# A graph, attention and expert block on one Trainium2 core: a new order in five places where stages meet

## What is computed

```python
xn = _layernorm(x)
x = x + gnn(xn, edge_index) + mix(xn)
x = x + ffn(_layernorm(x))
# gnn: layer_norm, two layers of graph attention (4 heads of 192, 2 heads of 96), then [x, out2] @ Wu + bu
#   e = leaky_relu(s_src[src] + s_dst[dst]); alpha = exp(e - max) / sum; out = sum(alpha * h[src])
# mix: linear attention with 12 heads of 64 (q, k = elu + 1), projection, then an MLP 768-3072-768
# ffn: router on the mean over all tokens, the two best of 4 experts (768-1536-768), gates, layer norm
```

## Time and profile before

| | |
|---|---|
| Runs of the kernel before | 1988.61 to 1995.7 us, median 1988.61 us (3 runs) |
| The profiled execution | 1991.11 us, its span 1989.4 us |
| TensorE busy | 1910.3 us, 96% |
| VectorE busy | 1179.5 us, 59% |
| ScalarE busy | 606.8 us, 31% |
| GpSimd busy | 415.9 us, 21% |
| Granted TensorE clock, mean | 0.981 of full speed |

### The profile page before, as it was taken

How to read it: one execution, slowest core, us unless ns; L and a number is a source line. 1 busy time by engine, 2 the same in 40 slices (tenths; PEclk the granted TensorE clock), 3 DMA queues, 4 the chain that set the end, 5 groups by cost and what they waited for, 6 DMA issues and landing times.

```text
span 1989.4 us, 28296 instructions
## 1 busy us (share of the span) xinstructions
PE 1910.3 (96%) x10979; PEld 1820.2 (91%) x10979; DVE 1179.5 (59%) x2085; ACT 606.8 (31%) x1175; POOL 415.9 (21%) x317
## 2 busy tenths in 40 slices
PE   7999899999789999999999999999989999999997
PEld 4677899999788999879999999999989999999997
DVE  8888569998784423678625334253557435274347
ACT  6533228888774311224401001010341001010013
POOL 1000001210000631133224124041114314043120
PEclk9999999999898999999999999999989999999999
DMA  4322401111123210023112011020232102021013
GB/s 146 118 95 102 132 7 50 60 42 48 74 117 145 87 48 1 25 67 114 55 41 64 16 48 56 9 64 17 66 92 64 40 25 65 9 79 40 25 52 120
DMA packets 76958, 125.50 MB, mean 63 GB/s; under 512 B 3350, under 2 KB 47672, under 8 KB 76830
## 3 DMA queue, kind: packets, MB, share of 16 engines
q1 hardware_dynamic: 73106, 111.22, 17.2%
q10 hardware_dynamic: 3724, 12.54, 1.7%
HBM read 98.30 MB, written 25.45 MB: 62 GB/s over the span
## 4 chain that ended last, share of the span: by engine, by line
PE 79%; DMA 7%; DVE 5%; ACT 4%; issue 2%; SPq 1%; ACTq 0%; POOL 0%; DVEq 0%; POOLq 0%
PE pb L1084 25%; PE pa L670 24%; PE pb L670 9%; PE pa L736 3%; PE pa L850 3%; PE pb L802 3%; PE pb L992 3%; PE pa L836 2%; DMA xg_d<-xw 2%; PE pb L850 2%; DMA xw<-wt_d 2%; DMA xu<-in_x 1%; DMA wt_d<-xu 1%; DMA md_d<-mds 1%; ACT sm L1483 1%
## 5 line engine op out<-in xcount | busy, mean ns | idle before, releaser
L1725 ACT ACTIVATE tr<-pb,V 128x418 f32<-128x418 f32 (+1 forms) x144 | 87.7, 610 | 765.3 <-PE pb L1084 762.5
L1084 PE MATMUL pb<-X_hi,uw_hi 128*128 128x416 f32 (+1 forms) x864 | 305.6, 354 | 3.2 <-DVE uw_lo L2324 3.2
L1084 PE MATMUL pb<-X_hi,uw_lo 128*128 128x416 f32 (+1 forms) x864 | 304.9, 353 | 0.0
L1084 PE MATMUL pb<-X_lo,uw_hi 128*128 128x416 f32 (+1 forms) x864 | 304.8, 353 | 0.0
L670 PE MATMUL pa<-dw_hi,hh 128*125 128x384 f32 x960 | 246.4, 338 | 0.7 <-ACT tr L1725 0.7
L670 PE MATMUL pa<-dw_hi,hl 128*125 128x384 f32 x960 | 245.9, 337 | 0.0
L670 PE MATMUL pa<-dw_lo,hh 128*125 128x384 f32 x960 | 245.9, 337 | 0.0
L2271 DVE CAST hh<-tr 128x418 fp32r<-128x418 f32 (+1 forms) x144 | 116.7, 811 | 202.6 <-ACT tr L1725 202.6
L1229 POOL CAST uw_hi<-raw 128x768 fp32r<-128x768 f32 x47 | 42.8, 911 | 708.8 <-PE pb L1084 612.3
L670 PEld LDWEIGHTS pa<-dw_hi,hh 128*125 128x125 f32 x960 | 172.2, 185 | 1.3 <-ACT tr L1725 1.0
L670 PEld LDWEIGHTS pa<-dw_lo,hh 128*125 128x125 f32 x960 | 172.9, 185 | 0.0
(11 more groups left out here) (396 smaller groups left out, 3547.0 us busy)
## 6 DMA issues: line engine op xcount, KB each, us to landing
raw<-in_L_mix_fc_w SPq DMA_DIRECT2D x48, 384.0 KB, 3.3
raw<-in_L_ffn_w SPq DMA_DIRECT2D x47, 384.0 KB, 3.2
md<-md_d SPq DMA_DIRECT2D x11, 610.4 KB
md_d<-mds SPq DMA_DIRECT2D x10, 610.4 KB
md<-md_d ACTq DMA_DIRECT2D x8, 610.4 KB
raw<-in_L_mix_qkv_w SPq DMA_DIRECT2D x24, 192.0 KB, 4.0
TOK<-in_x SPq DMA_DIRECT2D x10, 375.0 KB
xn_d<-TOK SPq DMA_DIRECT2D x10, 375.0 KB
```

The source lines that it names most:

```text
L1084: last = nc.tensor.matmul(pb[:, j % 4, 0:n], w_[:, kk, :], x_[:, kk, o:o + n], start=(kk == 0 and q == 0), stop=(kk == KT - 1 and q == 2))
L1725: last = A_(RE[f"tr{j % 3}"][:, 0:w], pb[:, j % 4, 0:w], ACT.Identity if func == "mish" else func, bias=bias(b))
```

## The change

It moves work in five places and computes the same values.

1. Edge stage: SyncE issues the load of `xu1` and `graph_tile` earlier in its loop; VectorE does `x_low(0)` after the one-hots of the next tile; the count of turns before a tile is added up in registers rather than loaded (`turns_before`).
2. Between the layers: steps 40 and 41 are done in two parts. `minus_max(s, 0)` on VectorE takes the maximum over the first 1125 columns, two one-column operations; ScalarE makes the weights of those columns with it (`weights_part`, signal `xa`), TensorE transposes and gathers them into a bank of their own (`weights_back_part`, `gather_part`, banks `early_sums`). When the last tile's scores are there, the last 125 columns are done with the final maximum (`tb`, `ev` signal the transpose and its copy), and `denominator_of_both` scales the early sums by a ratio, adds the late ones and takes the reciprocal: three operations.
3. Normed tiles: `xs` 0 and 1 are loaded right after layer 1, 2 and 3 by ScalarE's queue near the end of layer 2, the rest in the key stage; the rows `kvb` are loaded at the last two tiles. All ten are scaled by ScalarE. GpSimd waits for a key product before each page split.
4. Queries: nine jobs stand ahead, `q_sum` comes two jobs behind, the denominators of the first chunk after the eighth query, and GpSimd splits `wp` pages after jobs 5, 7, ... 15.
5. Router: the last tile's sums come from the unnormed tile (`scaled_sums`), and ScalarE copies the expert's page before `y_features(NT - 1)`; the gates are spread after the second expert job.

```diff
--- before.py
+++ after.py
             for t in range(NT):
-                if t >= XFIRST + 2:
-                    graph_tile(t - XFIRST - 2)
+                if t == 3:
+                    sp.wait_ge(*at("bu_ok", 1))
+                    sp.dma_start(RE["xu1"][:], x_t[1]).then_inc(sem("xu_in1"), 16)
                 for u in ln_tiles(t):
                     sp.wait_ge(*at("ln_xn", u + 1))
                     sp.dma_start(xn_d[u], TOK[:, u, :]).then_inc(sem("xn_out"), 16)
                 if t == 1:
                     for u in (0, 2):
                         sp.dma_start(RE[f"xu{u}"][:], x_t[u]).then_inc(sem(f"xu_in{u}"), 16)
-                if t == 3:
-                    sp.wait_ge(*at("bu_ok", 1))
-                    sp.dma_start(RE["xu1"][:], x_t[1]).then_inc(sem("xu_in1"), 16)
+                if t >= XFIRST + 1:
+                    graph_tile(t - XFIRST - 1)
                 sp.wait_ge(*at("e_md", t + 1))
                 sp.dma_start(md_d[t], RM[f"mds{t % 2}"][:]).then_inc(sem(f"md_out{t % 2}"), 16)
                 if t == XFIRST + 1:
                     for k in range(3):
                         rows_page(PG_W1 + k, A["gnn_W1"], k)
 
-            for u in range(NT - XFIRST - 2, NT):
+            for u in range(NT - XFIRST - 1, NT):
...
             sp.wait_ge(*at("at_o", STEPS1))
+            for t in range(2):
+                xs_load(t)
             for t in range(NT):
-                if t == NT - 2:
-                    xs_load(4)
+                if t >= NT - 2:
+                    g = t - NT + 2
+                    for v in range(2):
...
                 sp.wait_ge(*at("xg_ev", t + 1))
                 sp.dma_start(xg_d[t], RW[f"xw{t % 3}"][:]).then_inc(sem(f"xg_out{t % 3}"), 16)
                 if 1 <= t < NT - 2:
                     sp.wait_ge(*at(f"xg_out{(t - 1) % 3}", 16 * ((t - 1) // 3 + 1)))
                     sp.dma_start(RW[f"xw{(t - 1) % 3}"][:], wt_d[t + 2]).then_inc(sem(f"xw_in{(t - 1) % 3}"), 16)
-                if t < 4:
-                    xs_load(t)
-                elif t < 6:
-                    kvb_load(t - 4)
             for t in range(2, NT):
...
                 weights_back(i)
-                if i > 2:
+                if i == STEPS1 - 1:
+                    second_layer(NT - 2)
+                    gather(i - 1, lambda j: spread2(NT - 2) if j == NT // 2 else None)
+                elif i > 2:
                     gather(i - 1)
                 every(i, 5, H1, out1_back)
-                every(i, 7, H1, second_layer)
-            last_back(0)
-            gather(STEPS1 - 1, lambda j: spread2(NT - 2) if j == NT // 2 else None)
+                if i < STEPS1 - 1:
+                    every(i, 7, H1, second_layer)
+            gather(STEPS1 - 1, lambda j: last_back(0) if j == NT // 2 else None)
+            weights_back_part(0, 0)
+            last_back(1)
             pe.wait_ge(*at("o1_lo", NT))
             layer_products(NT - 1, blocks_of(0))
-            last_back(1)
             pe.wait_ge(*at("o1_lo", NT + 1))
             layer_products(NT - 1, blocks_of(1)).then_inc(sem("h2_mm"), 1)
-            spread2(NT - 1)
-            pe.wait_ge(*at("ssb2_ev", NT))
             pe.wait_ge(*at("g2_one", 1))
-            for i in range(STEPS1, STEPS):
+            gather_part(0, 0, lambda j: spread2(NT - 1) if j == NT // 2 else None)
+            weights_back_part(1, 0)
+            weights_back_part(0, 1)
+            gather_part(1, 0)
+            weights_back_part(1, 1)
+            gather_part(0, 1)
+            gather_part(1, 1)
+            for i in range(STEPS1 + 2, STEPS):
+                if i == STEPS1 + 2:
+                    pe.wait_ge(*at("ev1", 1))
                 weights_back(i)
-                if STEPS1 < i:
+                if STEPS1 + 2 < i:
...
             q_job(0)
             kv_product(2 * NT - 1)
-            for r in range(1, QRING):
+            for r in range(1, QRING + 1):
                 q_job(r)
                 if r == 3:
                     pe.wait_ge(*at("mats", 1))
                     q_sum(0)
-                    q_sum(1)
                 if r >= 3:
-                    q_sum(r - 1)
+                    q_sum(r - 2)
             for r in range(QLAST):
                 q_apply(r)
-                if r + QRING < QJOBS:
-                    q_job(r + QRING)
+                if r + QRING + 1 < QJOBS:
+                    q_job(r + QRING + 1)
...
-                pe.wait_ge(*at("y_xh", t + 1))
                 if t == NT - 1:
                     pe.wait_ge(*at("dn_acc", NT * MLP_GROUPS - 1))
-                    column_sums(pa[:, 0, :], t).then_inc(sem("y_sum"), 1)
+                    pe.wait_ge(*at("y_rs", t + 1))
+                    scaled_sums(pa[:, 0, :], t).then_inc(sem("y_sum"), 1)
                     router()
+                pe.wait_ge(*at("y_xh", t + 1))
...
+            def scaled_sums(bank, t):
+
+                for m in range(KT):
+                    nc.tensor.matmul(bank[:, m:m + 1], x2s[t % 3][:, m * P:(m + 1) * P], rs[:, 0, t:t + 1], start=(m == 0), stop=False,
+                                     skip_group_check=True)
+                return nc.tensor.matmul(bank[:, 0:KT], ones[0:TP, :], nm[:, t:t + 1].broadcast_to([TP, KT]), start=False, stop=True,
+                                        skip_group_check=True)
...
-                if n == 0:
+                if n == 1:
...
-            def norm_scale(t):
-                pool.wait_ge(*at(*normed_in(t)))
-                g_.tensor_scalar(normed(t)[:], normed(t)[:], rs[:, 2, t:t + 1], None, ALU.mult).then_inc(sem("xs_sc"), 1)
-
...
+            pool.wait_ge(*at("at_tr", 3 * STEPS))
+            for k in range(KT):
+                if k == 2:
                     pool.wait_ge(*at("wb_mm", NT))
                     for s in range(3):
                         pool.wait_ge(*at(f"xg_out{s}", 16 * len(range(s, NT, 3))))
-                if 2 <= t < 2 + KT:
-                    split_page(kv_page(1, t - 2), kvw[1][t - 2])
+                pool.wait_ge(*at("kv_mm", k + 1))
+                split_page(kv_page(1, k), kvw[1][k])
...
-                pool.wait_ge(*at("q_ap", 2 * k + 1))
+                pool.wait_ge(*at("qg_mm", 2 * k + 5))
...
             divided(STEPS1 - 2)
-            h2_out(NT - 2)
             last_high(0)
-            scores2_out(NT - 2)
+            weights_part(0, 0)
             divided(STEPS1 - 1)
+            above_part(1, 0)
             last_high(1)
-            act.wait_ge(*at("sn2", 1))
-            above_part(0)
+            back_out(STEPS1)
             h2_out(NT - 1)
+            weights_part(1, 0)
             scores2_out(NT - 1)
-            above_part(1)
-            least_above(STEPS1)
-            minus_max(STEPS1)
-            weights(STEPS1)
-            above(STEPS1 + 1)
...
+            above_part(0, 1)
+            above_part(1, 1)
+            weights_part(0, 1)
+            back_out(STEPS1 + 1)
+            weights_part(1, 1)
+            edge_load(0)
...
             def norm_scale(t):
 
-                if t < 4:
-                    act.wait_ge(*at(*normed_in(t)))
-                    A_(normed(t)[:], normed(t)[:], ACT.Copy, scale=rs[:, 2, t:t + 1]).then_inc(sem("xs_a"), 1)
-
-            for i in range(STEPS1, STEPS):
-                if STEPS1 + 2 <= i:
-                    divided(i - 2)
+                act.wait_ge(*at(*normed_in(t)))
+                A_(normed(t)[:], normed(t)[:], ACT.Copy, scale=rs[:, 2, t:t + 1]).then_inc(sem("xs_a"), 1)
+
+            for i in range(STEPS1 + 2, STEPS):
+                divided(i - 2)
                 every(i - STEPS1, 5, H2, out2_high)
-                if i + 1 < STEPS:
+                if STEPS1 + 2 < i < STEPS - 1:
                     least_above(i + 1)
                 every(i - STEPS1, 0, H2, edge_load)
-                every(i - STEPS1, 13, H2, norm_scale)
+                if i < STEPS1 + 12:
+                    every(i - STEPS1, 8, H2, norm_scale)
+                if i in (STEPS1 + 16, STEPS1 + 17):
+                    t = i - STEPS1 - 14
+                    act.dma_start(normed(t)[:], xn_d[t]).then_inc(sem(normed_in(t)[0]), 16)
...
+            norm_scale(2)
             x_out(1)
+            norm_scale(3)
...
+                if 4 <= n + 3 < NT:
+                    norm_scale(n + 3)
...
-            y_features(NT - 1)
             for q in range(2):
                 act.wait_ge(*at(f"x2_out{q}", 16 * len(range(q, NT, 3))))
             act.wait_ge(*at("pre_in", 16 * EXP))
             act.wait_ge(*at("r_idx", 1))
             first = act.value_load(rti[0:1, 0:1], min_val=0, max_val=EXP - 1)
             A_(uw[0][0][:], RE["pre"][:, ds(first, 1), :].rearrange("p e (k n) -> p (e k) n", k=KT), ACT.Copy).then_inc(sem("pre_hi"), 1)
+            y_features(NT - 1)
...
+                if t == XFIRST + 1:
+                    x_low(0)
...
-            denominator(STEPS1 - 2)
             scores2(NT - 2)
             dve.wait_ge(*at("g2_d", 1))
```

(34 more changed lines are left out.)

176 lines of the change are left out of this document (127 added, 49 removed).

## The result

The changed kernel takes 1982.22 us (median of 7 runs, 1980.34 to 1984.36), the kernel before, beside it, 1990.21 (1988.61 to 1995.7): a ratio of 0.9958, interval 0.9947 to 0.9969. The forecast was 1956, the range 1942 to 1976. The profiled executions are 1991.11 and 1980.34 us, their spans 1989.4 and 1978.6: 10.8 apart.

The account below looks back on a forecast made before the run. TensorE, working in 96% of the span, was taken as the bound, leaving idle time and low clock to win. 4.6 + 6.9 + 1.7 + 14.8 + 2.5 + 2.3 = 32.8 us off 1988.61 gave 1955.8; range 1942 to 1976.

Parts of the forecast that it names:

- graph, first half: Graph stage, 55 to 110: two TensorE waits shrink by 1.4 and 2.0 us, plus 1.2 of clock; 4.6 us, ends 3 and 6.
- graph, end: Graph stage, 200 to 242: the last xu load goes earlier, 5.2 us of wait and 1.7 of clock; 6.9, ends 3 and 8.5.
- between the layers: Crossing from layer 1 to 2: VectorE starts masking about 5 us earlier, 3.4 go back as extra work; +1.7, ends -4 and +5.
- tail and first keys: Layer 2's tail and first key tiles, 585 to 665: 7.7 and 1.1 us of idleness, 6.0 of clock; 14.8, ends 7 and 19.
- queries: Query stage, 810 to 885: 1.3 us of the last q_lo wait and 1.2 of clock; 2.5, ends -2 and 6.
- router: Router, 1464 to 1486: sums 1 us earlier, expert page copy 1.5 us; 2.3 taken, ends 0.5 and 6.
- The third term, 1.54: First key tiles: TensorE's 1.54 us wait for a kt of 2.17 us at 651.07, beside GpSimd's work, was to go.
- an end (7): Low end for layer 2's tail and first key tiles: margin gone, one wait stays, kvb loads come late; 7 us.
- rival (d): Key stage: SyncE's queue delays xs loads some 10 us for each of three pairs, late kvb another 5; 1993 us, chance 0.05.
- The low end, 3: End of the graph stage: the write of md_d[9], behind two transfers, holds up the W1 page; gain only 3 us.
- (c): Whole kernel: VectorE's added operations and new handovers eat the terms, leaving only the tail's two DMA waits; 1982 us, chance 0.08.
- rival (a): Layer 2's tail: the queues stay the bound and half that term goes; 1963.2 us, up to 1975, chance 0.15.

Follow-up runs that it names:

- the five kernels alike: The changed kernel and four follow-up kernels with the same query stage; the step from 660 to 930 is -0.1, -1.0, -1.3, +1.2 and -1.4.
- kvb_first: The changed kernel with the four kvb loads issued right after the first two xs loads; 1973.16 us, ratio 0.9915.
- two_parts_only: The kernel before with only steps 40 and 41 done in two parts; 1989.3 us, one execution.
- scale_in_gap: The changed kernel with a wait per kvb pair, first denominators after the seventh query, and ScalarE's first two xs scales at their step's head; 1965.52 us, 0.9864.
- splits_later: The changed kernel with GpSimd's splits of the wp pages waiting for the applied query jobs, as in the kernel before; 1980.55 us.

## Why the prediction was wrong, point by point

| term | forecast | measured | what it was |
|---|---|---|---|
| graph, first half | 4.6 | 2.8 | no gain from the clock |
| graph, end | 6.9 | 3.3 | bytes, not order |
| between the layers | 1.7 | 0.2, less 1.4 after it | VectorE's bound; scales on ScalarE |
| tail and first keys | 14.8 | 4.0; 12.3 to 13.7 with kvb mended | kvb issued late and waited for as a whole |
| queries | 2.5 | 0.1 (-1.2 to 1.4 in the five kernels alike) | later denominators, collision with a split, clock |
| router | 2.3 | 1.7 | |

**Tail and first key tiles**, most of the miss. The sum itself was nearly right: in kvb_first the stage gives 13.7 us from 570 to 770, and in the seven kernels that mend kvb without rows among the tiles `xw` 12.3 to 13.7 (the three with them 10.5 to 11.0). Of this up to 2 us may be the trace of the kernel before, as two_parts_only shows 1.9 there with nothing edited. The wait of 3.60 us of the earlier trace rows went, the one of 2.56, three tiles on, is still 1.90: VectorE has tile 4 in time, but waits for each `xw` tile from 5 to 8 (1.63, 2.16, 3.20 and 3.07 us), of which TensorE loses 1.90 and 0.50. So the queue's margin was there for the first tile that the prediction counted and not for the later ones. The third term, 1.54, isn't in the earlier trace rows; its row is

```profile
653.29 0.94 PE L954 MATMUL pa<-vt,kt 125*128 125x130 f32 x6 [1.54 <-DVE kt L2166]
```

and 0.79 of it is left in kvb_first, where one `kt` still takes 2.19 us.

The step that failed is the treatment of the kvb loads. I named them as an end (7) and in rival (d), and priced them at 5 us as a late landing. They cost 10: I had not asked what waits for them. VectorE's wait asks for all four at once, the last issue is 4 us later and the need 15 us earlier than in the kernel before, and behind the wait stands a chain of 8.9 us, which was hidden there. Rival (d) put its threshold at a landing of about 12 us, for the `xs` loads; the rows took 629.4 - 617.6 = 11.8 us from the last issue and 18 from the first, and no wait for an `xs` tile is among TensorE's large ones.

**End of the graph stage.** That the last load "is no longer last" was right, and "what is late next is the sixth page" too, but not by 2 us of spare. The load does go 13 us earlier (issued at 210.05 instead of 223.44). But from 198 to 224 us the transfers run without a gap, at about 130 GB/s and faster only while pages of 128 rows pass (157 in the mean of 197 to 222), and I let nothing move later for it. The low end, 3, with its reason (the buffers under `W1`) is what came.

**First half.** The idle time in the stretch fell from 6.6 to 52.20 - 48.97 = 3.2 us, the 3.4 that were forecast. The step that failed is the clock: it is 1.00 where it was 0.94, yet the stretch is only 2.8 us narrower, so of the deficit of 3.3, of which I took 1.2, nothing came. VectorE, which makes the one-hots, seems to set the pace there: it is busy 14.00 of 14.00 us from 56 to 70 in the changed kernel, and 8.00 of 8.00 from 82 to 90 in both. No run tests this.

**Between the layers.** The bound by VectorE held, and with it a gain near nothing. The waits of 2.09 and 2.16 us are the remainder of the crossing. Not priced at all were the scales on ScalarE, 1.3 us (scale_in_gap): I wrote that it is busy 31.54 of 80 us and took them for free. A free engine isn't a free place in its queue.

**Queries.** The last wait fell to 2.00 us, the forecast number, but not by the forecast's mechanism, which was 1.2 us more cover from the order of the sums. That it fits is luck. VectorE and GpSimd of the kernel before, at the last query:

```profile
871.70 1.02 DVE L2182 CAST q_hi<-qe 128x416 fp32r<-128x416 f32 x1
872.76 2.07 DVE L2183 TENSOR_TENSOR q_lo<-qe,q_hi 128x416 fp32r<-128x416 f32 x1
...
872.57 1.81 POOL L1230 TENSOR_TENSOR wp_lo<-raw,wp_hi 128x768 fp32r<-128x768 f32 x1
```

and VectorE of the changed kernel:

```profile
863.33 0.38 DVE L2319 CAST q_hi<-qe 128x416 fp32r<-128x416 f32 x1
863.74 0.59 DVE L2320 TENSOR_TENSOR q_lo<-qe,q_hi 128x416 fp32r<-128x416 f32 x1
```

Beside the split the two take 2.1 us more. In splits_later, with the new order but GpSimd's old gates, the last query is hit by as much (`qe` 1.21 us instead of 0.59, `q_hi` 1.86 instead of 0.38), and the wait is 4.08, not below 3.28. So the gates took the collision away, and of the cover by the order nothing is seen.

The first wait went up by 1.1 us, the collision that stood in the prediction as a sentence beside the sum. It kept a low stretch of the clock (0.63 from 811 to 815), and the one after the last wait grew: the clock's deficit from 810 to 885 rose from 5.2 to 74.70 x 0.09 = 6.7. That took the 1.3 us back.

**Router.** The sums come from the unnormed tile, and wait 0.81 us instead of 2.10; the wait for `uw_lo` is 2.36 us instead of 3.23.

```profile
1458.75 1.47 PE L1204 MATMUL pa<-rs,x2s 125*128 125x1 f32 x12 [0.81 <-DVE nm L2365]
...
1465.46 0.69 PE L1131 MATMUL pb<-X_hi,uw_hi 128*128 128x418 f32 x1 [2.36 <-DVE uw_lo L2460]
```

**The rivals.** The time is that of (c), 1982, but not by its mechanism: the gains of the graph stage, the tail and the router came, and one new wait took 10 us. With that wait and the denominators mended, the kernel stands at 1964, where rival (a) was, by chance: its mechanism, half of the tail's gain, isn't what is missing. Two of the signs that the prediction named against itself came: a DMA wait on `kvb`, and a split beside `z_hi`. The range was too narrow, since the terms did not miss independently: all six came out below their forecast, two (the graph's first half and the tail) below their low ends, and none above. Nearly every term was an idle time of the kernel before, with little or nothing taken off for the wait that follows it.

## What to carry to other kernels

When a load is moved later, read the wait that takes it: for how many loads it counts, and how long the chain behind it is up to the engine that sets the time. Split a wait for several loads when they are used at different times; it costs a semaphore and was worth about 10 us here. In a queue without gaps, as here at the end of the graph stage, reordering transfers changed which one was late; only fewer bytes moved the end. When a wait shrinks by the number that was forecast, still check which operation got shorter. Small work for a half-idle engine belongs where that engine waits, not ahead of what others wait for.
